# A graph network kernel: ACT and DVE swap two scalings, and the scatter takes its turn once for four groups

## The chip, the cores and the metric

The kernel runs on one core of a Trainium2 chip. The metric is the device time of one execution in microseconds (us). The engines are PE (TensorE, matrix products and transposes into PSUM), DVE (VectorE), ACT (ScalarE), POOL (GpSimd, here used for DMAs with an index per row) and SP (SyncE, here used to issue plain DMAs). Each engine works through its own instructions in order and waits on semaphores.

## The reference, cut to what matters

`x` has 100,000 rows of 128 numbers (f32). There are 25,000 edges, sorted by `dst`; `dst` is about 100,000 u^2 for uniform u, so the edges crowd at low rows.

```python
x = _layernorm(x + _L0_gnn_ref(x, edge_index, ...))   # edge MLP on x[src], x[dst]; segment_max over dst
x = _layernorm(x + _L1_gnn_ref(x, edge_index, ...))
# _L1: agg = segment_sum(x[src], dst); h = x + agg
#      res + relu(h @ W1 + b1) @ W2 + b2,  res = x @ Wres + bres
```

A row that is no edge's `dst` takes no part in the maximum or the sum: for it the two layers are plain dense products. A row that is a `dst` needs both.

## The kernel before

The kernel computes the whole output first as if no row were a `dst` (the dense work), computes the true rows of the `dst` rows in a second strand (the edge work), and lets POOL scatter these over the output rows that the dense work has stored.

**Dense work.** A unit is 512 rows (4 tiles of 128 rows, 128x512 f32). There are 196 units, four to a body, 49 bodies (0 to 48). For unit k the steps are: SP loads it into `x_in` (4 slots; slot k is loaded again when `x1_done` says that the unit in it has been scaled); DVE takes statistics (`bn_a`, `mv_a`), ACT the square root (`sd_a`), DVE the reciprocal (`rs_a`) and scales to `x1` (`norm1_scale`, L712, through the helper `scale`, L680); PE transposes to `psT`, ACT copies to `xT`; PE makes `psH`, ACT applies ReLU to `hT`; PE makes the rows in `psY` (2 buffers); DVE statistics (`bn_b`, `mv_b`), ACT root (`sd_b`), DVE reciprocal (`rs_b`), and ACT scales from `psY` to `o_rows` (`finish`, L1117, four instructions, one for each tile); SP stores. `psY` is free again at `o_done`. The layer norm needs no mean, since centring is folded into the weights. Units are pipelined: in step k DVE works on the second norm of unit k-3 and on the first norm of units k+1 to k+3, in the order that `dense` (L743) writes out.

**Edge work.** The edges are 49 groups of 512. `walk` (L310) puts each stage's edge steps beside dense units, the same for every engine:

- body 0 alone, then stage S (bodies 1 to 13, one edge step beside one unit, `step_s`): for each edge it finds where its source stands among the `dst` rows. Meanwhile POOL gathers the rows `x[src]` of groups 0 to 37 and `x[dst]` of groups 0 to 3 with indirect DMAs, four to a group.
- stage A (bodies 14 to 19, two edge steps beside one unit, an even and an odd one, `step_a`): the first layer, a running maximum, layer norm; the result goes to a table in DRAM, `x1e_table`. POOL gathers the other rows; the `dst` rows of group g wait for PE's transposes of group g-4.
- stage B (bodies 20 to 31, one edge step beside one unit, `step_b`): running sum, second layer, layer norm (`finish1`); results in `edge_rows`, counted by `res_done`. Before it can run, POOL must gather from `x1e_table`, 49 x 4 indirect DMAs (L586), which wait for the whole table.
- stage C (bodies 32 to 48): dense units alone.

After its gathers POOL scatters the 49 groups to `out` (L593), four indirect DMAs of 128 rows each to a group. Before group g it waits for `res_done` and, since the scatter must land on top of the dense rows, for the stores up to the body that holds the group's last `dst` row. That number comes from the data: `stores_16` has for each whole group 16 times this body's number, and `stores_needed` loads it into a register while the group before is scattered. After every second indirect DMA POOL waits for its descriptors to be written (`issued_pair`).

Of the kernel before, what the change touches and what calls it, by code (L numbers as in the profile page):

```python
# [36 lines left out]
TILES = 4  # L37
ROWS = TILES * P
SLOTS = 4
# [5 lines left out]
def gnn_program(nc, x, src, dst, e_w1, e_b1, e_w2, e_b2, w1, b1, w2, b2, wres, bres, out):  # L45
# [21 lines left out]
    with ctx:  # L67
# [47 lines left out]

        WHOLE = E // ROWS
        last_dst = sb("last_dst", [1, WHOLE], I32)
        stores_16 = sb("stores_16", [1, WHOLE], I32)

# [435 lines left out]
        def _(pool):  # L555
# [78 lines left out]
            def stores_needed(g):  # L634
                earlier = pool.value_load(stores_16[0:1, g:g + 1], min_val=0, max_val=16 * LAST)
                return pool.snap(earlier + 16)
# [3 lines left out]
            for g in range(GROUPS):  # L640
                j, r = divmod(g, SLOTS)
                wait(pool, final[r], 16 * TILES * j)
                pool.wait_ge(res_done, g + 1)
                if g < WHOLE:
                    for k in range(SLOTS):
                        pool.wait_ge(stored[k], count)
                    pool.nop().then_inc(s_turn, 1)
                elif g == WHOLE:
                    for k in range(SLOTS):
                        pool.wait_ge(stored[k], 16 * BODIES)  # L650
                for t in range(TILES):
# [8 lines left out]
        def _(dve):  # L660
# [50 lines left out]

            def norm1_scale(b, k):  # L712
                b, k = unit(b, k)
                if is_unit(b, k):
                    n = b * SLOTS + k
# [21 lines left out]
            def norm2_recip(b, k):  # L737
                b, k = unit(b, k)
                if is_unit(b, k):
                    dve.wait_ge(std2_done, b * SLOTS + k + 1)  # L740
                    v.reciprocal(rs_b[:, k, :], sd_b[:, k, :]).then_inc(rstd2_done, 1)  # L741

            def dense(b, k):  # L743
# [46 lines left out]
            def step_s(j, r, b):  # L790
                norm1_ready(b, r + 2)
                norm2_stats(b, r - 3)
                compare(j, r)
                norm1_var(b, r + 2)
                find(j, r - 2)
                norm2_ready(b, r - 3)
                norm1_scale(b, r + 1)
                norm2_var(b, r - 3)
                norm1_recip(b, r + 2)
                norm1_stats(b, r + 3, range(0, 2))  # L800
                norm2_recip(b, r - 3)
                norm1_stats(b, r + 3, range(2, TILES))
                keep_places(j, r - 3)
# [87 lines left out]
            def step_a(j, r, b, h):  # L891
# [9 lines left out]
                if b is not None and h % 2 == 0:  # L901
                    k = h // 2
                    norm1_ready(b, k + 2)
                    norm2_stats(b, k - 3)
                    norm1_var(b, k + 2)
                    norm1_scale(b, k + 1)
                if b is not None and h % 2 == 1:
# [3 lines left out]
                    norm2_var(b, k - 3)  # L911
                    norm1_stats(b, k + 3)
                    norm2_recip(b, k - 3)


# [46 lines left out]
            def step_b(j, r, b):  # L962
# [4 lines left out]
                if b is not None:  # L967
                    norm1_var(b, r + 2)
                    norm2_ready(b, r - 3)
                    norm1_scale(b, r + 1)  # L970
                    norm2_var(b, r - 3)
# [8 lines left out]
                if b is not None:  # L980
                    norm1_stats(b, r + 3)

# [21 lines left out]
            norm1_var(0, 1)  # L1004
            norm1_scale(0, 0)
            norm1_recip(0, 1)
# [70 lines left out]
        def _(act):  # L1077
# [54 lines left out]
            def second_half(b, k):  # L1132
                root2(b, k - 3)
                finish(b, k - 3)

# [88 lines left out]
            def step_b(j, r, b):  # L1224
# [6 lines left out]
                if b is not None:  # L1231
                    finish(b, r - 3)
                finish1(j, r - 2)

            root1(0, 0)
            root1(0, 1)
            act.wait_ge(s_w, 16 * 11)
            walk(act, dense, nothing, step_s, nothing, step_a, nothing, step_b)


# [231 lines left out]
```

## Time and profile before

| | before |
|---|---|
| median of 3 runs | 1345.21 us (1344.24 to 1346.85) |
| the profiled execution | 1332.02 us, of which 1330.2 us are the span from the first instruction to the last |
| busy: PE, DVE, ACT, POOL | 1123.7, 1068.6, 799.8, 825.8 us |
| granted clock of PE, mean | 0.952 of 2.4 GHz |
| moved by DMA | 233.86 MB, mean 176 GB/s |

Busy times are sums over stages with different limits, so none of them says by itself what sets the end. A row of the timeline is one instruction, or several of the same line that follow each other (x4); its first number is its start in us from the start of the span, the second its duration. "<-issue" is idle time for which the profile shows no other engine or transfer.

### The profile page before, as it was taken

How to read it: one execution, taken by the hardware profiler on the slowest of the kernel's cores; microseconds unless marked ns; L12 is line 12 of the kernel's file. 1: busy time of each engine (PE TensorE's matmuls, PEld its weight loads, DVE VectorE, ACT ScalarE, POOL GpSimd, SP SyncE). 2: the span in 40 equal slices, each digit the busy share in tenths (PEclk: the TensorE clock that was granted, in tenths of full speed). 3: DMA queues.
4: the chain of work that ended last, by engine and by line, in shares of the span. 5: the costliest groups of instructions: out<-in, count | busy, mean ns of one | idle time of the engine just before them, and what ended most of it. 6: DMA issues, size and time to landing. Idle time of an engine off the chain costs nothing. (4 is left out here: it accounts for less than half of the span.)

```text
span 1330.2 us, 32137 instructions
## 1 busy us (share of the span) xinstructions
PE 1123.7 (84%) x7512; PEld 853.2 (64%) x7512; DVE 1068.6 (80%) x5491; ACT 799.8 (60%) x2305; POOL 825.8 (62%) x797
## 2 busy tenths in 40 slices
PE   2699999998888878788759999999999999999500
PEld 1577777765555545455448888888887777777400
DVE  6599999989887887898838999999987888888400
ACT  0366666666665656667526666666666777777400
POOL 5666666656666666666256666666665666655654
PEclk9899999999998999999979999999999999999855
DMA  4477777756665667666436565656564556656310
GB/s 111 141 220 214 214 220 212 222 188 195 183 208 180 199 174 210 177 205 196 141 112 191 187 185 186 185 187 187 189 190 140 177 181 190 185 181 200 103 38 28
DMA packets 160366, 233.86 MB, mean 176 GB/s; under 512 B 26815, under 2 KB 69273, under 8 KB 160284
## 3 DMA queue, kind: packets, MB, share of 16 engines
q1 hardware_dynamic: 133612, 193.69, 46.7%
q0 software_dynamic: 25088, 38.81, 11.0%
q10 hardware_dynamic: 1584, 0.53, 0.2%
q14 instruction: 62, 0.51, 0.1%
q8 instruction: 20, 0.33, 0.1%
HBM read 129.48 MB, written 90.12 MB: 165 GB/s over the span
## 5 line engine op out<-in xcount | busy, mean ns | idle before, releaser
L1277 PE MATMUL psY<-wcr,xT 128*128 128x128 f32 x1568 | 305.0, 276 | 0.0
L1276 PE MATMUL psY<-wc,hT 128*128 128x128 f32 x1568 | 304.6, 276 | 0.0
L586 POOL DMA_INDIRECT edge_rows<-x1e_table,idx x196 | 210.8, 1075 | 133.2 <-DMA edge_rows<-x1e_table,idx 77.6
L593 POOL DMA_INDIRECT out<-edge_rows,idx x196 | 202.2, 1031 | 129.5 <-issue 76.4
L586 POOL DMA_INDIRECT edge_rows<-in_x,idx x196 | 206.9, 1056 | 116.0 <-DMA edge_rows<-in_x,idx 67.3
L586 POOL DMA_INDIRECT xd_rows<-in_x,idx x196 | 203.5, 1038 | 115.9 <-DMA xd_rows<-in_x,idx 67.3
L1276 PEld LDWEIGHTS psY<-wc,hT 128*128 128x128 f32 x1568 | 255.8, 193 | 15.0 <-issue 8.3
L1123 ACT ACTIVATE o_rows<-psY,rs_b 128x128 f32<-128x128 f32 x784 | 223.0, 367 | 66.7 <-DVE rs_b L741 66.5
L1277 PEld LDWEIGHTS psY<-wcr,xT 128*128 128x128 f32 x1568 | 239.9, 193 | 0.0
L1287 PE MATMUL psH<-xT,wc 128*128 128x512 f32 x392 | 204.5, 604 | 16.0 <-DVE deltas L787 10.6
L1103 ACT ACTIVATE sd_a<-mv_a,eps_col 128x4 f32<-128x4 f32 x196 | 58.3, 298 | 239.6 <-DVE mv_a L677 239.6
L672 DVE BATCH_NORM_STATS2 bn_b<-psY 128x6 f32<-128x128 f32 x784 | 174.4, 285 | 21.9 <-PE psY L1277 7.9
L691 DVE BATCH_NORM_STATS2 bn_a<-x_in 128x6 f32<-128x128 f32 x784 | 173.1, 271 | 0.3 <-DMA x_in<-in_x 0.3
L1267 PEld LDWEIGHTS psT<-ident,x 128*128 128x128 f32 x784 | 99.5, 143 | 106.2 <-issue 104.9
L1092 ACT ACTIVATE hT<-psH,bias_cols 128x512 f32<-128x512 f32 x196 | 131.0, 669 | 5.0 <-PE psH L1287 5.0
L682 DVE TENSOR_TENSOR x<-x_in,rs_a 128x512 f32<-128x512 f32 x196 | 130.6, 666 | 0.3 <-PE psT L1267 0.3
L1267 PE MATMUL psT<-ident,x 128*128 128x128 f32 x784 | 119.5, 276 | 0.9 <-DVE idx L1055 0.9
L1267 PE MATMUL psE<-ident,xs_rows 128*128 128x128 f32 x392 | 61.8, 281 | 60.8 <-ACT ehT L1161 51.6
L1100 ACT COPY xT<-psT 128x512 f32<-128x512 f32 x196 | 112.5, 574 | 0.5 <-PE psT L1267 0.5
L1267 PEld LDWEIGHTS psE<-ident,xs_rows 128*128 128x128 f32 x392 | 45.9, 143 | 98.2 <-issue 83.0
L923 DVE TENSOR_TENSOR_SCAN shared<-mask,shared,psE 128x512 f32<-128x512 bf16 x48 | 61.4, 1279 | 36.5 <-PE psE L1267 23.5
L1287 PEld LDWEIGHTS psH<-xT,wc 128*128 128x128 f32 x392 | 65.8, 194 | 35.6 <-issue 11.0
(135 smaller groups left out, 2042.6 us busy)
## 6 DMA issues: line engine op xcount, KB each, us to landing
x_in<-in_x SPq DMA_DIRECT2D x196, 256.0 KB
out<-o_rows SPq DMA_DIRECT2D x196, 256.0 KB
xs_rows<-edge_rows SPq DMA_DIRECT2D x98, 256.0 KB, 2.9
xs_rows<-src_dram SPq DMA_DIRECT2D x49, 256.0 KB, 4.3
mask<-mask_dram SPq DMA_DIRECT2D x98, 128.0 KB, 3.6
x1e_table<-shared SPq DMA_DIRECT2D x49, 256.0 KB, 2.8
x1eT_spill<-x1eT SPq DMA_DIRECT2D x49, 256.0 KB
x1eT<-x1eT_spill SPq DMA_DIRECT2D x49, 256.0 KB, 2.8
```

Source lines behind the costliest of these rows:

```text
L586: nc.gpsimd.indirect_dma_start(to, None, table, bass.IndirectOffsetOnAxis(idx[:, what, t:t + 1], 0), bounds_check=rows - 1, oob_is_err=err ...
L593: nc.gpsimd.indirect_dma_start(table, bass.IndirectOffsetOnAxis(idx[:, SCAT, t:t + 1], 0), frm, None, bounds_check=N - 1, oob_is_err=False ...
L672: last = v.bn_stats(bn[:, t, :], rows[:, cut(t)])
L682: v.tensor_tensor(tiles(to), tiles(rows), rs.unsqueeze(2).broadcast_to([P, TILES, P]), ALU.mult).then_inc(done, 1)
L691: last = v.bn_stats(bn_a[:, k % 2, t, :], x_in[:, k, cut(t)])
L1092: a.activation(hT[:, k % 2, :], psH[:, :], ACT.Relu, bias=bias_cols[:, 2:3]).then_inc(hT_done, 1)
L1100: a.copy(xT[:, k, :], psT[:, :]).then_inc(xT_done, 1)
L1123: last = a.activation(o_rows[:, k, cut(t)], psY[k % 2][:, cut(t)], ACT.Copy, scale=rs_b[:, k, t:t + 1])
L1267: last = t_.transpose(to[:, cut(t)], rows[:, cut(t)], ident[:, :])
L1276: t_.matmul(to[:, cut(t)], h[:, cut(t)], wc2[:, :], start=False, stop=False, skip_group_check=True)
L1277: last = t_.matmul(to[:, cut(t)], xt[:, cut(t)], wcr[:, :], start=False, stop=t == TILES - 1, skip_group_check=True)
L1287: t_.matmul(psH[:, :], wc1[:, :], xT[:, k, :], start=True, stop=True).then_inc(w1_done, 1)
```

## The change

Two edits. First, the scalings are swapped. ACT now makes `x1` from `x_in` with four instructions, after the root for the second norm; DVE now makes `o_rows` from `psY` with one instruction (`scale`), at the end of its step, after the reciprocal `rs_b`. The statistics of the next unit move up to where DVE's scaling stood. Second, POOL's scatter takes its turn (the four waits on `stored`, the nop, and the register load) only at every fourth group, with the count of the last group of the four.

```diff
             def stores_needed(g):
-                earlier = pool.value_load(stores_16[0:1, g:g + 1], min_val=0, max_val=16 * LAST)
+                top = g + SLOTS - 1
+                earlier = pool.value_load(stores_16[0:1, top:top + 1], min_val=0, max_val=16 * LAST)
                 return pool.snap(earlier + 16)
...
                 pool.wait_ge(res_done, g + 1)
-                if g < WHOLE:
+                if g < WHOLE and r == 0:
                     for k in range(SLOTS):
                         pool.wait_ge(stored[k], count)
                     pool.nop().then_inc(s_turn, 1)
...
                 for t in range(TILES):
-                    if t == TILES - 1 and g + 1 < WHOLE:
+                    if t == TILES - 1 and r == SLOTS - 1 and g + 1 < WHOLE:
                         count = stores_needed(g + 1)
```

DVE:

```diff
-            def norm1_scale(b, k):
-                    dve.wait_ge(rstd1_done, n + 1)
-                    wait(dve, t_done, n - 1)
-                    scale(x1[:, k % 2, :], x_in[:, k, :], rs_a[:, k, :], x1_done)
+            def finish(b, k):
+                    dve.wait_ge(rstd2_done, b * SLOTS + k + 1)
+                    wait(dve, stored[k], 16 * b)
+                    scale(o_rows[:, k, :], psY[k % 2], rs_b[:, k, :], o_done)
 
             def dense(b, k):
                 norm1_ready(b, k + 2)
                 norm2_stats(b, k - 3)
                 norm1_var(b, k + 2)
                 norm2_ready(b, k - 3)
-                norm1_scale(b, k + 1)
+                norm1_stats(b, k + 3, range(0, 1))
                 norm2_var(b, k - 3)
                 norm1_recip(b, k + 2)
-                norm1_stats(b, k + 3, range(0, 2))
+                norm1_stats(b, k + 3, range(1, TILES))
                 norm2_recip(b, k - 3)
-                norm1_stats(b, k + 3, range(2, TILES))
+                finish(b, k - 3)
```

`step_s`, `step_a` and `step_b` of DVE are changed in the same way: in stage A two of the four statistics take the scaling's place in the even step, and `finish` comes last in the odd step; in stages S and B `finish` comes after the last statistics (in S ahead of `keep_places`). The first `norm1_scale(0, 0)` moves to ACT too.

ACT:

```diff
-            def finish(b, k):
-                    act.wait_ge(rstd2_done, b * SLOTS + k + 1)
-                    wait(act, stored[k], 16 * b)
+            def norm1_scale(b, k):
+                    act.wait_ge(rstd1_done, n + 1)
+                    wait(act, t_done, n - 1)
                     for t in range(TILES):
-                        last = a.activation(o_rows[:, k, cut(t)], psY[k % 2][:, cut(t)], ACT.Copy,
-                                            scale=rs_b[:, k, t:t + 1])
-                    last.then_inc(o_done, 1)
+                        last = a.activation(x1[:, k % 2, cut(t)], x_in[:, k, cut(t)], ACT.Copy,
+                                            scale=rs_a[:, k, t:t + 1])
+                    last.then_inc(x1_done, 1)
...
             def second_half(b, k):
                 root2(b, k - 3)
-                finish(b, k - 3)
+                norm1_scale(b, k + 1)
```

## Rows read from the trace of the kernel before

**Rows 1.** Windows of three stretches: us, each engine's busy time and count, granted clock, DMA.

```profile
668.00:990.00 322.00, 307.85 (x2103) 254.06 (x2102) 271.07 (x1362) 203.36 (x632) 210.76 (x196) 0.97 0.57 179
990.00:1255.00 265.00, 255.71 (x1729) 202.03 (x1727) 222.75 (x1374) 201.35 (x603) 161.59 (x155) 1.00 0.56 175
1255.00:1331.00 76.00, 0.00 (x0) 0.00 (x0) 0.00 (x0) 0.00 (x0) 40.58 (x42) 0.50 0.11 33
```

**Rows 2.** Waits of the whole span: in total, times, longest us.

```profile
POOL edge_rows L586 <- DMA x1e_table<-shared: 22.8, 1, 22.8
DVE bn_z L672 <- PE psE L1267: 21.1, 25, 1.7
```

**Rows 3.** Timeline of POOL near the end: start, us, [idle before <-releaser].

```profile
1290.21 0.98 POOL L593 DMA_INDIRECT out<-edge_rows,idx  x1 [1.10 <-issue]
...
1309.49 0.98 POOL L593 DMA_INDIRECT out<-edge_rows,idx  x1 [1.08 <-issue]
...
1315.65 0.98 POOL L593 DMA_INDIRECT out<-edge_rows,idx  x1 [0.81 <-DMA out<-edge_rows,idx]
```

**Rows 4.** Timeline of DVE and POOL in stage C.

```profile
1094.20 0.89 DVE L672 BATCH_NORM_STATS2 bn_b<-psY 128x6 f32<-128x128 f32 x4
...
1095.29 0.69 DVE L682 TENSOR_TENSOR x<-x_in,rs_a 128x512 f32<-128x512 f32 x1
...
1095.43 1.41 POOL L593 DMA_INDIRECT out<-edge_rows,idx  x1 [0.81 <-DMA out<-edge_rows,idx]
...
1096.98 0.18 DVE L741 RECIPROCAL rs_b<-sd_b 128x4 f32<-128x4 f32 x1 [0.28 <-ACT sd_b L1103]
...
1097.65 0.49 DVE L672 BATCH_NORM_STATS2 bn_b<-psY 128x6 f32<-128x128 f32 x2
```

**Rows 5.** Timeline of DVE and POOL in stage B, early and late.

```profile
694.71 0.69 DVE L934 TENSOR_TENSOR xsT<-shared,x1eT 128x512 f32<-128x512 f32 x1
...
694.86 1.41 POOL L586 DMA_INDIRECT edge_rows<-x1e_table,idx  x1 [0.30 <-issue]
...
894.04 0.66 DVE L934 TENSOR_TENSOR xsT<-shared,x1eT 128x512 f32<-128x512 f32 x1
...
894.57 1.00 POOL L586 DMA_INDIRECT edge_rows<-x1e_table,idx  x1 [0.81 <-DMA edge_rows<-x1e_table,idx]
...
897.58 0.66 DVE L682 TENSOR_TENSOR x<-x_in,rs_a 128x512 f32<-128x512 f32 x1
...
897.67 1.43 POOL L586 DMA_INDIRECT edge_rows<-x1e_table,idx  x1 [0.81 <-DMA edge_rows<-x1e_table,idx]
```

**Rows 6.** Timeline of DVE and POOL in stage A.

```profile
594.42 0.20 DVE L855 RECIPROCAL rs_e<-sd_e 128x8 f32<-128x8 f32 x1
...
594.66 0.69 DVE L682 TENSOR_TENSOR shared<-psE,rs_e 128x512 f32<-128x512 f32 x1
594.85 1.01 POOL L586 DMA_INDIRECT xd_rows<-in_x,idx  x1 [0.79 <-DMA xd_rows<-in_x,idx]
...
595.29 1.28 DVE L876 TENSOR_TENSOR_SCAN shared<-mask,shared,psE 128x512 f32<-128x512 bf16 x1
```

**Rows 7.** Timeline of DVE over one unit of stage S.

```profile
201.09 0.89 DVE L672 BATCH_NORM_STATS2 bn_b<-psY 128x6 f32<-128x128 f32 x4
...
204.88 0.18 DVE L741 RECIPROCAL rs_b<-sd_b 128x4 f32<-128x4 f32 x1
204.98 0.46 DVE L691 BATCH_NORM_STATS2 bn_a<-x_in 128x6 f32<-128x128 f32 x2
...
205.56 0.89 DVE L672 BATCH_NORM_STATS2 bn_b<-psY 128x6 f32<-128x128 f32 x4
```

**Rows 8.** Groups of ACT by form: busy, mean ns | idle before.

```profile
L1123 ACT ACTIVATE o_rows<-psY,rs_b 128x128 f32<-128x128 f32 x784 | 223.0, 367 | 66.7 <-DVE rs_b L741 66.5 <-issue 0.2
...
L1178 ACT ACTIVATE edge_rows<-xs_rows,rs_e 128x128 f32 x128 | 41.0, 400 | 0.0
```

**Rows 9.** DMA issues: KB each, median us to landing.

```profile
x1eT<-x1eT_spill SPq DMA_DIRECT2D x49, 256.0 KB, 2.8
```

More of the change, by code:

```diff
@@ L116, in gnn_program @@
         WHOLE = E // ROWS
+        assert WHOLE % SLOTS == 0
         last_dst = sb("last_dst", [1, WHOLE], I32)
@@ L710, in norm1_recip @@
                     v.reciprocal(rs_a[:, k, :], sd_a[:, k, :]).then_inc(rstd1_done, 1)
-            def norm1_scale(b, k):
-                b, k = unit(b, k)
-                if is_unit(b, k):
-                    n = b * SLOTS + k
-                    dve.wait_ge(rstd1_done, n + 1)
-                    wait(dve, t_done, n - 1)
-                    scale(x1[:, k % 2, :], x_in[:, k, :], rs_a[:, k, :], x1_done)
             def norm2_stats(b, k):
@@ L741, in norm2_recip @@
                     v.reciprocal(rs_b[:, k, :], sd_b[:, k, :]).then_inc(rstd2_done, 1)
+            def finish(b, k):
+                b, k = unit(b, k)
+                if is_unit(b, k):
+                    dve.wait_ge(rstd2_done, b * SLOTS + k + 1)
+                    wait(dve, stored[k], 16 * b)
+                    scale(o_rows[:, k, :], psY[k % 2], rs_b[:, k, :], o_done)
             def dense(b, k):
@@ L796, in step_s @@
                 norm2_ready(b, r - 3)
-                norm1_scale(b, r + 1)
+                norm1_stats(b, r + 3, range(0, 1))
                 norm2_var(b, r - 3)
                 norm1_recip(b, r + 2)
-                norm1_stats(b, r + 3, range(0, 2))
+                norm1_stats(b, r + 3, range(1, TILES))
                 norm2_recip(b, r - 3)
-                norm1_stats(b, r + 3, range(2, TILES))
+                finish(b, r - 3)
                 keep_places(j, r - 3)
@@ L905, in step_a @@
                     norm1_var(b, k + 2)
-                    norm1_scale(b, k + 1)
+                    norm1_stats(b, k + 3, range(0, 2))
                 if b is not None and h % 2 == 1:
@@ L911, in step_a @@
                     norm2_var(b, k - 3)
-                    norm1_stats(b, k + 3)
+                    norm1_stats(b, k + 3, range(2, TILES))
                     norm2_recip(b, k - 3)
+                    finish(b, k - 3)
             def segment_sum(j, r):
@@ L969, in step_b @@
                     norm2_ready(b, r - 3)
-                    norm1_scale(b, r + 1)
+                    norm1_stats(b, r + 3, range(0, 1))
                     norm2_var(b, r - 3)
@@ L980, in step_b @@
                 if b is not None:
-                    norm1_stats(b, r + 3)
+                    norm1_stats(b, r + 3, range(1, TILES))
+                    finish(b, r - 3)
             v.memset(eps_col[:, :], EPS)
@@ L1004, in _ @@
             norm1_var(0, 1)
-            norm1_scale(0, 0)
             norm1_recip(0, 1)
@@ L1115, in root2 @@
                     root(sd_b[:, k, :], mv_b[:, k, :, :], std2_done)
-            def finish(b, k):
+            def norm1_scale(b, k):
                 b, k = unit(b, k)
                 if is_unit(b, k):
-                    act.wait_ge(rstd2_done, b * SLOTS + k + 1)
-                    wait(act, stored[k], 16 * b)
+                    n = b * SLOTS + k
+                    act.wait_ge(rstd1_done, n + 1)
+                    wait(act, t_done, n - 1)
                     for t in range(TILES):
-                        last = a.activation(o_rows[:, k, cut(t)], psY[k % 2][:, cut(t)], ACT.Copy,
-                                            scale=rs_b[:, k, t:t + 1])
-                    last.then_inc(o_done, 1)
+                        last = a.activation(x1[:, k % 2, cut(t)], x_in[:, k, cut(t)], ACT.Copy,
+                                            scale=rs_a[:, k, t:t + 1])
+                    last.then_inc(x1_done, 1)
             def first_half(b, k):
@@ L1231, in step_b @@
                 if b is not None:
-                    finish(b, r - 3)
+                    norm1_scale(b, r + 1)
                 finish1(j, r - 2)
@@ L1236, in _ @@
             root1(0, 1)
+            norm1_scale(0, 0)
             act.wait_ge(s_w, 16 * 11)
```

## The prediction

> **What bounds the kernel now.** I read the windows first, then who waited for whom, then POOL's and DVE's timelines side by side. The reader should see that dense work doesn't set the end. From 1255 us on PE, DVE and ACT are idle, and only POOL's indirect DMAs run, 42 of them [rows 1]. Before that POOL runs its 196 gathers from the edge table back to back from 668 to 990, and its 196 scatters follow without a pause [rows 1]. It last waited long for others at 668, 22.8 us for the table's stores [rows 2]; in the code it also waits for stage A's first transposes before it gathers further `dst` rows. So the span is: the end of stage S (it lets stage A begin), stage A up to the table's last store, and then 392 indirect DMAs of POOL. Dense units after 668 only have to stay ahead of the scatters.
>
> A POOL issue has a natural price. With nothing beside it it takes 0.98 us, the next pair follows after 0.81 us, and the next group of four after 1.08 us; only at the last group is that 0.81 too, though it waits for the four `stored` counts, as constants [rows 3]. In the gathers it is 1.00, with 0.30 inside a pair [rows 5]. While DVE works, some issues last longer. In stage C one that starts 0.14 us into `x<-x_in,rs_a` lasts 1.41 [rows 4]; in stage B one that starts 0.09 us into it lasts 1.43 [rows 5]. Both end 0.86 us after DVE's instruction does (1096.84 against 1095.98, 899.10 against 898.24): POOL's issue stands until DVE is through.
>
> **The change, part by part.**
>
> *One turn for four groups.* Of the 49 scatter groups, 36 lose four register waits, the nop, and the register load ahead of them. If their gap goes from 1.08 to 0.81 [rows 3], that is 36 x 0.27 = 9.7 us, all on POOL's chain. Bounds: zero if the `res_done` wait, which stays, carries the cost, and 9.7. The last group has that wait too, at 0.81, so I take 9.7. In return the first group of each four waits for the output rows of the group three further on. The latest such turn is group 44's, at 1290.2 [rows 3]; it would need what edge 24575 needs: row 100000 x (24576/25000)^2 = 96,600, body 47 (bodies 0 to 48). Dense work was over before 1255 [rows 1], and body 47 four units of 3.45 us earlier [rows 4], near 1240. That cover is 50 us; what eats it comes below.
>
> *DVE's x1 scaling goes, and POOL is freed of it.* What replaces it on DVE reads PSUM and one small SBUF operand. Stage A has that form now: a POOL issue that starts 0.19 us into `shared<-psE,rs_e` lasts 1.01 us, not lengthened [rows 6]. So `finish` should not hold POOL. In stage C the lengthening is 161.59 - 155 x 0.98 = 9.7 us [rows 1], and nothing else in a dense unit reads two SBUF tensors: -9.7. Bounds: 0 (the PSUM form blocks too) and -12, a quarter more, since gaps beside it may be stretched as well.
>
> In stage B it is 210.76 - 196 x 1.00 = 15 us [rows 1], but I don't book it. Four gathers take by nature 4 x 1.00 + 0.30 + 0.81 + 0.30 + 0.81 = 6.2 us; POOL took 322/49 = 6.57 us [rows 1], and that is also the pitch of a step of stage B, which PE fills (307.85 us busy of 322). POOL is being held to DVE's period: each step it comes 0.37 us earlier, runs into `x<-x_in,rs_a`, and is pushed back by as much. Stage B has a second instruction with two SBUF tensors, `xsT<-shared,x1eT` (L934), and that lengthens too: an issue 0.15 us into it lasted 1.41 [rows 5]. Today POOL starts 0.53 us into it and just escapes, at 1.00 [rows 5]. With the first blocker gone POOL slides 0.37 us earlier and falls into the second, which at 0.66 us is long enough to hold it for good. At most five steps pass until one of four starts meets it: 5 x 0.37 = 1.9 us. I take -2; bounds 0 and -15.
>
> Here a rule can be weighed. The rows show issues escaping or being held until DVE's end, and where they fall isn't chance but a slide [rows 5]. The Trainium skill, "SBUF — State Buffer", section "Who interferes with whom", says that a DVE instruction with two SBUF inputs contends with a GpSimd instruction that reads SBUF, and that the one to start second blocks fully; it says nothing of who meets whom. Were POOL's starts spread at random, the 0.66 us left in each step would cost 4 x 0.66/6.57 x 0.33 = 0.13 us a group, 6.5 us in all, and stage B would gain 9 us rather than 2. By that reading the time would be 7 us lower.
>
> *DVE in stage S.* Its instructions stand back to back; a unit takes 201.09 to 205.56 = 4.47 us [rows 7]. It pays 0.69 us for the PSUM form and loses 0.66 for the SBUF one [rows 5, 6]. `finish` also waits for the reciprocal just ahead of it: that step is 0.24 us in stage A [rows 6], against 0.10 from the reciprocal to the next statistics now [rows 7]. Together +0.17 us. Against it, the wait of the next step for DVE's own last statistics (205.44 to 205.56) would be met early: up to -0.15. So +0.02 to +0.17 a unit, over 52 units +1 to +9. I take +3, since the gap that goes is seen directly. The reverse, a shorter stage S, would need PE to be faster, and PE is full there too; I give it no weight.
>
> *ACT.* Four scalings from SBUF at 0.40 us each take the place of four from PSUM at 0.37 [rows 8], some 0.1 us a unit. ACT was busy 201 of 265 us in stage C [rows 1], less elsewhere, and no longer waits for `rs_b`. Cost 0; if ACT had no slack, 196 x 0.1 = 20 us. x1 is there some 2 us later in its step; PE transposes it a step later, which covers that.
>
> *Stage A.* 0. DVE waited 21.1 us in 25 places, 0.84 each, for `bn_z`'s input [rows 2]; `finish` comes just ahead of those, after two statistics fewer. The even steps' chain, DVE's `mv_a` to ACT's root, ReLU and copy, is untouched. Without that cover: 24 x 0.63 = 15 us.
>
> *Stage C's dense work* gets longer, off the path. A unit is 1094.20 to 1097.65 = 3.45 us, in a loop from `bn_b` through ACT to `rs_b` and in 0.67 us back to `bn_b` [rows 4]. That leg becomes 0.24 + 0.63 = 0.87 [rows 6], so 3.65 a unit; 68 units add 14 us. Body 47 is stored near 1240 + 14 + 3 (stage S) + 3 (landing) = 1260. POOL comes to group 44 at 1290.2 - 9.7 - 2 - 33 x 0.27 + 3 = 1273. 13 us are left: hidden.
>
> **Sum.** -9.7 (turn) - 9.7 (stage C) - 2 (stage B) + 3 (stage S) = -18.4 us. The profiled execution took 1332.0 us; the runs shown have a median of 1345.2, 13 us above it, an offset that I let stand. 1345.2 - 18.4 = 1326.8, say 1326.
>
> **Rivals.**
> 1. *POOL runs free in stage B too.* For: L934 hits it rarely so far. Against: those hits look the same. 13 us more; POOL is then at group 44 at 1260, just as body 47's rows land: 1313. Chance 0.13.
> 2. *Stage S slows by 0.3 us a unit*, DVE waiting for `std2` behind ACT's queue. For: ACT's root comes after ReLU and copy. Against: three statistics, not two, now lie in that wait. 52 x 0.3 = 16 instead of 3: 1339. Chance 0.13.
> 3. *The PSUM form blocks POOL as well*, so half of the change doesn't do what I say. Against: rows 6. -9.7 and +3 are left: 1338. Chance 0.07.
> 4. *Slower: the stores become the end.* Place: group 44's turn. x1 releases its input slot 2 us later, the reload comes late, and a unit of stage C stretches beyond 3.65. From 3.85 (0.2 x 64 = 13 us) POOL waits, from 4.15 the gain is gone, at 4.3 it is 1326 + 29 = 1355. For: the reload keeps about 4.4 us, two units less the 3 by which it is late. Against: other transfers of this size land in 2.8 [rows 9]. Chance 0.06.
> 5. *Stage A pays for `finish` in full and more*, 24 x 1 us: 1350. Against: the waits in front of `bn_z`. Chance 0.06.
>
> The forecast case has 0.5, with its own range of 1318 to 1332; 0.05 is left for what I don't see. A measurement of this kernel tells about 0.2%, 2.7 us, from no change. Faster by more: 0.5 + 0.13 + 0.12 (of case 2) + 0.06 and a little of the rest, 0.82; within: 0.06; slower: 0.12. The range takes in cases 1 to 3: 1310 to 1341.
>
> **What would show it.** Right: scatter gaps of 1.08 at every fourth group and 0.81 at the others; issues of 1.0 us through stage C; in stage B still 6.6 us a group, the long issues now beginning inside L934; stage S 1 to 9 us longer; a dense unit of stage C near 3.65. Wrong: gathers at 6.2 us a group (case 1), a unit of stage S over 4.7 (2), POOL's issues lengthened inside `o_rows<-psY` (3), POOL waiting for `out<-o_rows` at group 44 (4), the table's last store more than 10 us after 668 with stage S unchanged (5).

## The result and the profile after

| | time, us | kernel before, same chip | ratio, 95% |
|---|---|---|---|
| the change, first measured | 1383.01 (1373.12 to 1387.28, 4 runs) | 1346.03 | 1.0274 (1.0219 to 1.0328) |
| the change, measured again later (e11) | 1331.60 (1328.67 to 1334.96, 10 runs) | 1334.28 | 0.9981 (0.9967 to 0.9995) |

The change was slower by 2.7% when it was first measured, where 1326 us was forecast. The same kernel on another occasion was 0.2% faster than the kernel before. Both are true, and most of this document is about what lies between them: TensorE's semaphore updates, which on some occasions arrive microseconds late.

The first profiled execution took 1383.84 us, 1381.8 of them span. Windows of it over stage B, the dense part of C, and the end (columns as in [rows 1]):

```profile
715.00:1089.00 374.00, 333.27 (x2231) 268.41 (x2230) 288.67 (x1453) 221.63 (x678) 237.15 (x236) 0.98 0.54 164
1089.00:1334.00 245.00, 228.85 (x1474) 171.12 (x1473) 197.60 (x1218) 174.03 (x512) 124.83 (x127) 1.00 0.55 168
1334.00:1381.00 47.00, 13.88 (x99) 11.37 (x97) 11.98 (x60) 8.18 (x22) 19.67 (x20) 0.69 0.19 65
```

Before, DVE and PE were through at 1255 and POOL went on alone [rows 1]. Now dense work runs past 1334, and in its last part POOL does little. Its waits (in total, times, longest) and its timeline say why:

```profile
POOL out L594 <- DMA out<-o_rows: 56.1, 3, 53.9
POOL edge_rows L587 <- DMA x1e_table<-shared: 36.4, 1, 36.4
DVE bn_y L675 <- remote: 30.3, 23, 3.1
DVE bn_b L675 <- remote: 18.7, 18, 2.3
```

```profile
1287.69 0.98 POOL L594 DMA_INDIRECT out<-edge_rows,idx  x1 [0.50 <-issue]
1342.58 0.98 POOL L594 DMA_INDIRECT out<-edge_rows,idx  x1 [53.91 <-DMA out<-o_rows]
1343.86 0.98 POOL L594 DMA_INDIRECT out<-edge_rows,idx  x1 [0.30 <-issue]
```

That is the turn of group 44: POOL stood 53.9 us for output rows that dense work had not stored. What POOL itself does became shorter, as the change meant. What became longer is everything that PE feeds. Where the stages begin (first `hT<-psH` of the stage, first and last indirect DMA, us from the span's start):

| | before | after | after again (e11) | turn, exchange in C alone, marks (e17) |
|---|---|---|---|---|
| stage S | 59.8 | 64.9 | 63.9 | 59.9 |
| stage A | 301.9 | 320.8 | 309.7 | 302.9 |
| stage B | 684.1 | 715.5 | 704.2 | 688.3 |
| stage C | 1016.6 | 1089.4 | 1038.6 | 1023.6 |
| first gather from the table | 668.2 | 699.8 | 689.1 | 672.5 |
| first scatter | 991.4 | 1009.7 | 1009.6 | 996.8 |
| last scatter | 1320.0 | 1371.6 | 1316.9 | 1305.0 |
| span | 1330.2 | 1381.8 | 1327.0 | 1315.2 |

Stage B took 373.9 us instead of 332.5. Its unit was 6.6 us before; now, but for one, units of 6.1 to 9.5 follow each other without order. By its own execution stage C began 72.8 us later than before: the start of stage S gave 5.1 of it, stage S 13.8, stage A 12.5 and stage B 41.4. "<-remote" in the waits is a semaphore update that fits the end of no instruction in the profile. It stands only at waits for what PE makes, on DVE above all (`bn_b`, `bn_y`). The table was ready late too, 36.4 us of waiting for 22.8 [rows 2].

**How a late update looks.** The trace has the time of a semaphore update beside the end of the instruction that carries it. In the first profile of before, all 1053 updates of PE that stages S to C show lie within 0.04 us of that end. After the change, of those recorded, 141 of 236 in stage S, 6 of 183 in A, 180 of 260 in B and 46 of 154 in C come more than 0.3 us behind the last matmul that carries one, up to 5.6 us; those of ACT and DVE are never over 0.01 us late. A piece of experiment e3, from the trace (start, duration, instruction; `update` rows are semaphores):

```
1210.57 0.28 PE  last matmul psY<-wcr,xT  (carries y_done)
1211.66      PE  psH<-xT,wc, ends 1212.78 (carries w1_done)
1212.95 0.27 PE  last transpose of psT    (carries t_done)
1212.97      update x1_done (ACT, on time)
1215.15      update y_done   4.31 us behind its matmul
1215.18 0.30 DVE bn_b<-psY
1215.19      update w1_done  2.41
1215.25      update t_done   2.03
```

PE worked on: the product and the transposes behind the late one are in the record, and a product of 1.12 us can't have been done in the 0.04 us between the first two updates. So it is the word of the work that is late, and it comes in a bunch. It isn't only the time noted for it: DVE, which waits for this update, starts 0.03 us after that time. All that comes behind DVE's first wait stands too:

```profile
1212.14 0.69 DVE L685 TENSOR_TENSOR o_rows<-psY,rs_b 128x512 f32<-128x512 f32 x1
1215.18 0.50 DVE L675 BATCH_NORM_STATS2 bn_b<-psY 128x6 f32<-128x128 f32 x2 [2.34 <-remote]
```

**Missing records go with it.** The six traces without a late update (before, e8 to e11, e17) hold 29,921 to 30,676 semaphore updates, those of the DMAs included. The 13 with many late ones hold 12,335 to 14,139, and e7 holds 19,886. Records of every engine are missing. In stage C they are missing only while POOL issues: in those 13 traces 62% to 73% of the updates of PE, DVE and ACT are there then, and practically all while POOL waits. So what delays PE's updates also loses records, or the recording is itself what delays them. Every execution on record has its span and granted clock noted, so no run here tells the two apart.

### The profile page after: what moved, and what is told of

It is laid out like the page before. It is cut to its first block and busy times, and to the rows that moved or that the text cites. A ratio compares the mean times of both kernels' runs of the same rounds, so it can differ in the third digit from the quotient of the medians.

```text
span 1381.8 us, 31908 instructions
## 1 busy us (share of the span) xinstructions
PE 1171.4 (85%) x7512; PEld 861.5 (62%) x7512; DVE 1082.8 (78%) x5491; ACT 807.2 (58%) x2305; POOL 797.4 (58%) x797
## 5 line engine op out<-in xcount | busy, mean ns | idle before, releaser
L1281 PE MATMUL psY<-wc,hT 128*128 128x128 f32 x1568 | 308.5, 279 | 0.0
L594 POOL DMA_INDIRECT out<-edge_rows,idx x196 | 194.3, 991 | 170.7 <-issue 94.3
L587 POOL DMA_INDIRECT edge_rows<-x1e_table,idx x196 | 197.3, 1007 | 146.8 <-issue 90.2
L1281 PEld LDWEIGHTS psY<-wc,hT 128*128 128x128 f32 x1568 | 259.8, 196 | 19.6 <-issue 11.6
L587 POOL DMA_INDIRECT edge_rows<-in_x,idx x196 | 201.6, 1029 | 116.0 <-issue 73.6
L1127 ACT ACTIVATE x<-x_in,rs_a 128x128 f32<-128x128 f32 x784 | 249.5, 394 | 0.0
L694 DVE BATCH_NORM_STATS2 bn_a<-x_in 128x6 f32<-128x128 f32 x784 | 179.5, 271 | 5.1 <-DMA x_in<-in_x 5.0
L1272 PEld LDWEIGHTS psT<-ident,x 128*128 128x128 f32 x784 | 91.3, 143 | 147.3 <-issue 91.8
L685 DVE TENSOR_TENSOR o_rows<-psY,rs_b 128x512 f32<-128x512 f32 x196 | 134.8, 688 | 9.6
L1095 ACT ACTIVATE hT<-psH,bias_cols 128x512 f32<-128x512 f32 x196 | 131.6, 671 | 12.5 <-PE psH L1292 6.4
L1272 PE MATMUL psT<-ident,x 128*128 128x128 f32 x784 | 125.2, 283 | 14.3 <-ACT x L1127 6.6
```

What stands on the lines that cost most here:

```text
L587: nc.gpsimd.indirect_dma_start(to, None, table, bass.IndirectOffsetOnAxis(idx[:, what, t:t + 1], 0), bounds_check=rows - 1, oob_is_err=err ...
L594: nc.gpsimd.indirect_dma_start(table, bass.IndirectOffsetOnAxis(idx[:, SCAT, t:t + 1], 0), frm, None, bounds_check=N - 1, oob_is_err=False ...
L685: v.tensor_tensor(tiles(to), tiles(rows), rs.unsqueeze(2).broadcast_to([P, TILES, P]), ALU.mult).then_inc(done, 1)
L694: last = v.bn_stats(bn_a[:, k % 2, t, :], x_in[:, k, cut(t)])
L1095: a.activation(hT[:, k % 2, :], psH[:, :], ACT.Relu, bias=bias_cols[:, 2:3]).then_inc(hT_done, 1)
L1127: last = a.activation(x1[:, k % 2, cut(t)], x_in[:, k, cut(t)], ACT.Copy, scale=rs_a[:, k, t:t + 1])
```

## The experiments

Late updates are given as "late/recorded" for stages S, B and C (C to the end of the span), from the one profiled execution of each kernel. "Chip" is the median of the kernel before in the same batch on the same chip. An occasion with late updates is called disturbed here, one without them quiet. Where no ratio stands, the kernel's own runs spread too far for one (e0 is a single run).

| | kernel | us | chip | ratio, 95% | S | B | C |
|---|---|---|---|---|---|---|---|
| e1 | turn alone | 1359.2 | 1365.6 | 0.995 (0.991 to 0.998) | 148/238 | 146/252 | 6/184 |
| e2 | exchange alone | 1421.0 | 1365.6 | | 176/250 | 191/257 | 38/137 |
| e3 | after, x1 first | 1489.6 | 1365.6 | | 164/246 | 213/271 | 53/183 |
| e4 | after, reciprocal apart | 1475.7 | 1365.6 | 1.081 (1.077 to 1.084) | 157/235 | 182/263 | 74/188 |
| e0 | before | 1339.5 | 1340.4 | | 119/216 | 115/241 | 14/186 |
| e5 | after, both on DVE | 1351.3 | 1340.4 | 1.009 (1.006 to 1.012) | 61/208 | 26/207 | 21/183 |
| e6 | after, both on ACT | 1373.7 | 1340.4 | 1.028 (1.022 to 1.034) | 152/219 | 120/228 | 54/160 |
| e7 | after, pause behind each issue | 1498.6 | 1340.4 | 1.118 (1.113 to 1.124) | 27/198 | 0/208 | 0/135 |
| e8 | after, mark on each issue | 1332.2 | 1334.3 | 0.999 (0.997 to 1.001) | 0/257 | 0/290 | 0/198 |
| e9 | turn, mark on each issue | 1331.0 | 1334.3 | 0.997 (0.996 to 0.998) | 0/251 | 0/290 | 0/202 |
| e10 | after, pause in the scatters | 1388.2 | 1334.3 | 1.041 (1.039 to 1.043) | 0/260 | 0/290 | 0/199 |
| e11 | after | 1331.6 | 1334.3 | 0.998 (0.997 to 1.000) | 0/261 | 0/290 | 0/196 |
| e12 | turn, exchange in C alone | 1408.9 | 1365.0 | 1.034 (1.029 to 1.039) | 149/234 | 156/250 | 75/187 |
| e13 | exchange alone | 1424.6 | 1365.0 | 1.046 (1.040 to 1.052) | 165/243 | 180/269 | 41/143 |
| e14 | after, A as before | 1466.4 | 1365.0 | 1.073 (1.067 to 1.079) | 159/235 | 215/269 | 55/190 |
| e15 | turn alone | 1361.3 | 1365.0 | 0.999 (0.995 to 1.003) | 163/242 | 132/241 | 6/193 |
| e16 | as e12 | 1396.6 | 1362.1 | | 134/229 | 124/239 | 91/176 |
| e17 | as e12, mark on each issue | 1314.0 | 1334.7 | 0.985 (0.983 to 0.986) | 0/260 | 0/290 | 0/201 |

### First batch: which edit, and is x1 or DVE's scaling late?

e1 and e2 are the two edits of the change, each alone. e3 moves ACT's job to the head of its step; it still makes unit k+1 there, so it comes a step earlier:

```diff
             def first_half(b, k):
+                norm1_scale(b, k + 1)
                 root1(b, k + 2)
...
                 root2(b, k - 3)
-                norm1_scale(b, k + 1)
```

e4 puts work between DVE's reciprocal and the scaling that waits for it:

```diff
-                norm1_stats(b, k + 3, range(1, TILES))
+                norm1_stats(b, k + 3, range(1, 3))
                 norm2_recip(b, k - 3)
+                norm1_stats(b, k + 3, range(3, TILES))
                 finish(b, k - 3)
```

e1: 

> The kernel before, with the scatters turning once for four groups and no job exchanged. Both theories below put the loss on the exchange of jobs, so both expect what the prediction's term for the turn says: 36 turns less of about 0.27 us, 9.7 us, so 1333 to 1338 us. A rival: the turn moved to the first group of four asks for stores that land up to four groups later, so that the last turn (group 44) waits for the dense stores also without the exchange. Then 1342 us or more, and the trace shows a wait of POOL of several us at group 44.

e2: 

> The kernel after, with a turn for every group as before. If the exchange is what costs, 1375 to 1393 us (the kernel after, with at most 10 us more, and nothing more if POOL waits for stores at the end anyway). If the turn is what costs (its wait asks for stores of later groups), about 1336 us.

e3: 

> The kernel after, with ACT scaling x1 as the first thing of its step instead of the last. Theory X (x1 comes just in time for TensorE's transposes, and TensorE, full in stages S and B, loses each wait): TensorE's waits on ACT's x1 (61 us in 95 pieces) vanish, stage S's unit of 5.6 us in each loop turn goes back to 4.5, stage B's unit to near 6.6, total about 1320 to 1340 us. Theory D (it is DVE's output scaling from PSUM at the end of its step, behind its own reciprocal, that delays y's buffer and DVE's next step): no more than 10 us are won, 1372 to 1383 us, and stage B's unit stays at 7.5 or more.

e4: 

> The kernel after, with DVE's reciprocal of norm 2 one statistics instruction earlier in the dense steps and in stage S, so that its output scaling doesn't wait for the instruction just ahead of it. Theory D: the unit of 5.6 us in each loop turn of stage S and the irregular units of stage C shrink, 1360 to 1372 us. Theory X: nothing changes, 1378 to 1388 us.

The kernel before took 1365.6 us on this chip, 20 more than in the first measurement. The turn is innocent (0.995), the exchange costs. All four took longer than expected, on a base that was itself 20 us higher. The wait that e1's rival names is there:

```profile
POOL out L594 <- DMA out<-o_rows: 4.1, 1, 4.1
```

But e1 has 148 late updates in stage S and 146 in B, and its stage C began at 1090.1 us, 73.5 later than in the profile of before: dense work came late to the turn, not the turn early. Both theories of the exchange's cost fell: x1 a step earlier took PE's waits for it away and the kernel still became slower, and so did the one with the reciprocal apart. Neither touches anything that could cost 50 to 70 us. What they have in common is DVE waiting for "remote", in total, times, longest, in e3:

```profile
DVE bn_b L675 <- remote: 91.2, 58, 3.2
DVE bn_y L675 <- remote: 44.1, 28, 3.1
```

The update times above came out of looking for that. e3 also shows when they are on time. In its stage C, windows of one unit each:

```profile
1206.01:1210.46 4.45, 4.34 (x33) 3.59 (x32) 3.14 (x21) 2.71 (x9) 2.94 (x3) 1.00 0.66 174
1210.46:1216.59 6.13, 3.94 (x27) 2.99 (x25) 3.15 (x22) 2.71 (x10) 3.93 (x4) 1.00 0.58 188
1307.64:1311.23 3.59, 3.57 (x25) 2.81 (x25) 3.05 (x21) 2.71 (x8) 0.00 (x0) 1.00 0.52 146
1311.73:1315.47 3.74, 3.63 (x26) 2.88 (x25) 3.11 (x21) 2.71 (x9) 0.00 (x0) 1.00 0.54 145
```

While POOL issues (fifth busy time above 0), a unit takes 3.6 to 6.1 us. POOL waits for the stores twice, 35.6 us ahead of group 40 (from 1294) and 94.1 us ahead of group 44; there (POOL at 0.00) all units but the first take 3.59 to 3.73 us until the work runs out. Of the 105 updates of PE recorded more than 1.5 us into these two waits none is late. It is the same in all ten traces with such a wait of over 4 us (the kernel after, e1 to e4, e6, e12 to e14, e16): 0 of 556.

### Second batch: is it the kernel before's too, and what brings it?

e0 is the kernel before. e5 is the kernel after with `norm1_scale` on DVE in its old place, so DVE has both scalings; e6 has `finish` back on ACT, behind `norm1_scale`. e7 makes POOL wait for each of its issues:

```diff
-                if issued[0] % 2 == 0:
-                    kw["engine_sem"] = s_issued
+                kw["engine_sem"] = s_issued
...
-                if issued[0] % 2 == 0:
-                    pool.wait_ge(s_issued, issued[0] // 2)
+                pool.wait_ge(s_issued, issued[0])
```

e0: 

> The kernel before once more, on this chip, for its trace. New theory L: TensorE's semaphore updates arrive late (by 1 to 8 us, several in one bunch) while GpSimd issues its indirect DMAs, and each late one holds DVE and ACT; the exchange makes this more frequent, the queue itself is not slower. If the kernel before suffers from it too and only its first profiled execution was free of it, this trace has some 150 late updates in each of stages S and B and nearly none in C, and the time is 1345 to 1370 us, not 1332. If lateness comes only with the changed kernels, it has none.

e5: 

> The kernel after with x1's scaling back on DVE at its old place: DVE has both scalings, ACT neither. If it is DVE's two-operand read of SBUF (which lengthens GpSimd's issues and locks their rhythm to the units) that keeps TensorE's updates in time in stage C, this kernel has few late updates there (under 10 of some 180), while its unit is set by DVE at 3.9 to 4.2 us; total 1375 to 1400 us. If the scaling of the output on DVE brings the lateness, C has 40 or more late updates here as after the change.

e6: 

> The kernel after with the output scaling back on ACT, behind x1's: ACT has both, DVE neither. ACT is then full (stage C's unit about 4.3 us by ACT's 2.7 us and 1.6 us more, stage B's about 7), total 1400 to 1440 us. If the freed GpSimd is the source of the lateness, late updates of TensorE stay in stage C (30 or more) though DVE no longer touches the output; if DVE's scaling is the source, there are under 10.

e7: 

> The kernel after, but GpSimd waits for the end of each indirect issue, not of every second one: a group of four goes from 6.2 to about 7.2 us, so stages B and C can be held by GpSimd, but it is quiet for longer. Theory L: the late updates come out in the pause behind a pair (0.5 to 0.8 us after its end in two of three cases), so with a pause behind each issue the longest delays fall from 5 to 6 us to under 3, the units of S and B become more even, and the total is 1340 to 1375 us. If the lateness has nothing to do with GpSimd's issuing, the total is 1383 us or more.

The kernel before has late updates too, in S and B, and hardly in C: its first profiled execution (1332.0 us) had none, and the median of its other runs was 13 us above. e0's 1339.5 us lie below the 1345 to 1370 expected. e5 is better than expected (1351.3 us, not 1375 or more): DVE sets the unit (S 4.91, C 3.83 us, nearly all alike), PE has time left in each, and fewer updates are late, 21 of 183 in C, which is between the two cases that I had set. e6 was faster than expected too, and has 54 of 160 late in C although ACT scales the output, so DVE's PSUM scaling is not what brings them; what e6, the kernel after, and e2 to e4 share is that x1's scaling has left DVE. e7's total was missed by far: 7.2 us a group was too slow for the gathers of stages A and B (A took 463 us). But its late updates are as theory L says: none in A, B and C, and none over 1.2 us in S. The occasion was a disturbed one all the same, since records are missing here too: only 208 of PE's 290 updates in B and 135 of 202 in C are there, where all but a few are in the traces of quiet occasions. So the lateness can be kept away while whatever loses the records goes on. Units of C are 3.58 to 3.75 us with POOL issuing beside them:

```profile
1202.06 0.98 POOL L592 DMA_INDIRECT out<-edge_rows,idx  x1 [0.81 <-DMA out<-edge_rows,idx]
1203.86 0.98 POOL L592 DMA_INDIRECT out<-edge_rows,idx  x1 [0.81 <-issue]
```

### Third batch: the mark or the pause, and stage C

e8 and e9 keep e7's first edit (each issue marks its end) and wait for every second one; e8 from the kernel after, e9 from before with the turn. e10 has e7's pause in the last 196 issues alone. e11 is the kernel after.

e8: 

> The kernel after, with GpSimd marking the end of every indirect issue (as the run that waited for each issue did) but waiting only for every second one (as the kernel after does). It separates the mark from the pause. If it is the pause behind each issue that lets TensorE's updates through, this kernel is as late as the kernel after: 100 or more late updates in each of S and B, its time within 1.5% of the kernel after. If it is the mark, the late updates are gone in A, B and C at GpSimd's full pace of 6.2 us a group, and the time falls to 1310 to 1340 us.

e9: 

> The kernel before with one turn for four groups and every issue marked, waiting for every second one. If the pause matters and not the mark: as the turn alone, 0.993 to 0.997 of the kernel before. If the mark matters: 0.975 to 0.985, since late updates cost the kernel before some 25 us in S and B.

e10: 

> The kernel after, with GpSimd waiting for each issue in the scatters alone (last 196 of its 784); the gathers keep their pairs. Theory L: stage C's units become even (3.59 to 3.75 us, mean 3.65 against 3.85) with no late update there, S and B stay as late as in the kernel after; 68 units by 0.2 us are 13 us, and GpSimd's 49 groups of 7.2 us end just as the dense stores do, so 1365 to 1378 us where the kernel after takes 1383. If lateness comes from elsewhere, C stays uneven and the time is 1383 us or more.

e11: 

> The kernel after once more, on the chip of these runs, so that traces and times of one chip can be compared. Theory L: 1.02 to 1.04 of the kernel before, again with late updates of TensorE above all in S and B, and some 40 in C.

This was the chip of the first batch, 25 minutes later, and nothing was late in any of the four, so e11 missed its 1.02 to 1.04. The kernel before took 1334.3 us on it, not 1365.6. So the lateness isn't the chip's, nor the kernel's alone: something that changes with time turns it on. Mark against pause couldn't be told apart. e10 shows the bare price of the pause, 365.6 us of scatters for 307.3, and gains nothing where nothing is late (1388.2 us, above the range expected).

e11 is the measurement of the change that the prediction can be held against step by step. In stage B a gather that starts 0.14 us into `xsT<-shared,x1eT` is held:

```profile
803.75 0.66 DVE L937 TENSOR_TENSOR xsT<-shared,x1eT 128x512 f32<-128x512 f32 x1
...
803.89 1.38 POOL L587 DMA_INDIRECT edge_rows<-x1e_table,idx  x1 [0.81 <-DMA edge_rows<-x1e_table,idx]
```

In stage C nothing holds an issue, and the unit is 3.60 to 3.75 us:

```profile
1095.09 0.69 DVE L685 TENSOR_TENSOR o_rows<-psY,rs_b 128x512 f32<-128x512 f32 x1
1095.36 0.98 POOL L594 DMA_INDIRECT out<-edge_rows,idx  x1 [0.81 <-DMA out<-edge_rows,idx]
```

Stage A is where the gain goes. Two of its units each in e9 (A's jobs as before) and in e11:

```profile
426.89:441.60 14.71, 12.46 (x69) 8.27 (x67) 13.12 (x60) 9.93 (x28) 9.53 (x10) 1.00 0.66 203
441.60:456.38 14.78, 12.42 (x69) 8.29 (x67) 13.08 (x60) 9.86 (x27) 10.07 (x10) 1.00 0.66 198
```

```profile
438.72:455.05 16.33, 14.18 (x67) 9.41 (x67) 13.28 (x60) 10.10 (x28) 10.86 (x11) 0.90 0.60 186
455.05:469.83 14.78, 12.60 (x67) 8.21 (x67) 13.26 (x60) 9.97 (x27) 9.36 (x9) 1.00 0.65 200
```

The unit of 16.33 us has a granted clock of 0.90, the others 1.00, and PE is busy 1.6 us longer over the same work. PE's timeline, e9 and then e11, has the idle time ahead of it:

```profile
440.73 1.04 PE L1269 MATMUL psE<-ident,shared 128*128 128x128 f32 x8
443.47 0.63 PE L1269 MATMUL psE<-ident,xs_rows 128*128 128x128 f32 x4 [1.71 <-ACT ehT L1163]
```

```profile
437.46 1.09 PE L1272 MATMUL psE<-ident,shared 128*128 128x128 f32 x8
440.60 0.63 PE L1272 MATMUL psE<-ident,xs_rows 128*128 128x128 f32 x4 [2.05 <-ACT ehT L1165]
441.07 0.63 PE L1272 MATMUL psE<-ident,xd_rows 128*128 128x128 f32 x4
441.54 1.50 PE L1386 MATMUL psE<-ehT,raw 128*128 128x512 f32 x2
```

PE's longest wait in two steps, for ACT's ReLU, is 1.71 us in e9 and 2.05 in e11. After it, in e11, the granted clock falls to 0.5 (1.2 GHz) and two products take 1.50 us instead of 1.02. Of e11's 20 waits of 1.88 to 2.05 us at this place 12 are followed by such a fall; of the 37 of 1.47 to 1.78 us in e9 and before none is. Stage A has 17 such stretches in e11, 68 us together, against 5 with 27 us in e9 and 6 with 34 in before. The sizes fit. From one first `hT<-psH` to the next, nine of e11's 24 units in stage A take 16.25 to 16.66 us, each with one fall, and one each in e9 and before; most others take 14.6 to 15.0 us in all three. Eight units by 1.6 us are 13 us, and stage A grew by 12.4. e5 and e6 tell which half of the exchange does it: with DVE scaling the output (e5) 16 stretches, with ACT doing both (e6) 5, and stage A took 389.3 and 383.4 us.

### Fourth and fifth batch: the exchange in stage C alone

e12 has the turn, and the exchange in the dense steps after body 0 alone; e14 is the kernel after with both jobs in stage A as before. e13 and e15 are e2 and e1 again.

```diff
             def dense(b, k):
+                late = not (isinstance(b, int) and b == 0)
...
-                norm1_scale(b, k + 1)
+                if late:
+                    norm1_stats(b, k + 3, range(0, 1))
+                else:
+                    norm1_scale(b, k + 1)
```

e12: 

> The kernel before with the turn for four groups, and the exchange of jobs in the steps of stage C alone; S, A and B as before. Theory K (the exchange costs in A by TensorE's clock, in S and B by fuller queues, and gives in C by GpSimd's freed issues): scatters begin where they did before (about 992 us), take 307 us as after the change and not 326, so the span is 1309 us and the time 1311 us, ratio 0.980 to 0.986 on a quiet chip. If the gain in C hangs on something in the other stages, 0.995 or more. With late updates of TensorE (a kernel before above 1340 us): 0.985 to 1.005, since C's units then have 13 us of slack before the turn of group 44.

e13: 

> The exchange alone, a turn for every group, once more on this chip. Quiet chip: the kernel after and 36 turns more of 0.27 us, so 1339 to 1343 us, ratio 1.003 to 1.008; stage A has 10 or more stretches of half clock. With late updates: 1.03 to 1.05 as at first.

e14: 

> The kernel after with stage A's jobs as in the kernel before. Theory K: stage A goes from 394.6 us back to 382, with 5 or fewer stretches of half clock, and the time falls by 10 to 13 us to 1319 to 1322 us, ratio 0.988 to 0.991 on a quiet chip. If A is slow for another reason (x1 late, more work on DVE in S), it stays at 390 us or more and the ratio at 0.998.

e15: 

> One turn for four groups alone, once more on this chip. In the run with marks GpSimd's groups in stage C stayed at 6.87 us, two units of DVE, since DVE's two-operand scaling holds the issues to the units' rhythm, and the turn's 9.7 us were mostly lost to longer issues (54 over 1.2 us, not 14). So 0.995 to 0.998, not 0.993.

Here the kernel before took 1365.0 us, and updates were late again. e12 is then 1.034, outside the range I gave: stage C alone had 75 of 187 updates late, all before POOL stood at group 44.

```profile
POOL out L594 <- DMA out<-o_rows: 83.9, 2, 82.8
DVE bn_b L675 <- remote: 77.0, 49, 3.9
```

Beside it e15, the same kernel but for stage C's jobs, had 6 of 193 late in C and units of 3.36 to 3.49 us, one excepted. That pair shows what the exchange does in C when updates can be late. e14's stage A fell from e13's 12 stretches of half clock to 7, but took 394.0 us against 394.9. It had more late updates in A too (46 of 215 against 25 of 198), so it doesn't settle A. The turn alone is worth little, since POOL's groups stay at two units of DVE, 6.9 us, with 55 issues held over 1.2 us.

e16: 

> The exchange in stage C alone with the turn for four groups, once more. Quiet chip (kernel before at 1331 to 1338 us): S, A and B as in the kernel before, scatters of 307 us in place of 326, time 1311 to 1318 us, ratio 0.980 to 0.988, no late update. Disturbed chip (kernel before at 1350 us or more): 1.03 again, with uneven units in C while GpSimd issues and even ones while it waits.

e17: 

> The exchange in stage C alone, the turn for four groups, and a mark on every indirect issue with a wait for every second one. Quiet chip: 1311 to 1318 us, ratio 0.980 to 0.988. Disturbed chip: if the pause behind each issue is what helps, stage C is uneven as in the two runs before (ratio 1.02 to 1.04, 40 or more late updates in C); if the mark is, C is even (3.59 to 3.75 us) and the ratio 0.98 to 1.00.

e16 met late updates again (1396.6 us for 1362.1, about 1.025). e17 met none and gave 0.985 (0.983 to 0.986), the version that the experiments pointed to, within the 1311 to 1318 us expected. Its windows, stage B, dense C, end:

```profile
684.00:1023.00 339.00, 328.61 (x2247) 269.93 (x2247) 289.59 (x1462) 219.52 (x682) 221.37 (x206) 0.98 0.57 178
1023.00:1270.00 247.00, 238.53 (x1570) 180.95 (x1568) 205.28 (x1266) 181.05 (x533) 153.65 (x157) 1.00 0.57 177
1270.00:1315.00 45.00, 0.59 (x6) 0.40 (x4) 2.92 (x12) 0.41 (x2) 23.15 (x24) 0.55 0.14 44
```

It beats the kernel before when updates are on time, and by its ratio the kernel after too. Its marks have no part in that: the kernel after gave 0.999 with them (e8) and 0.998 without (e11). With late updates only the version without marks was seen, and it was as bad as the change (e12, e16). So neither can be called the better kernel without knowing how often that is, and e17's own time with late updates is not known.

## Why the prediction was wrong

**What failed for the first measurement: the base.** "13 us above it, an offset that I let stand": I took the difference between the profiled execution (1332.0 us) and the median (1345.2) for a constant. It was most likely the kernel's own loss to late updates. The profiled execution had none. Where traces show none, the kernel before had medians of 1334.3 and 1334.7 us; where they show many, 1340.4 to 1365.6. For the executions behind 1345.2 there is no trace, so for them this is inferred. And the loss is no constant, it grows when x1's scaling leaves DVE: the kernel after takes 1383.0 us with late updates and 1331.6 without, 51 us where before has 12 (1346.0 against 1334.3).

**And the overlap.** "Dense units after 668 only have to stay ahead of the scatters", with 13 us left at group 44, "hidden", and nothing booked for it. The forecast let stage C begin 3 us later and gave it units of 3.65 us. It began 72.8 us later, and its first 56 units took 3.85 us on average. POOL was ready for group 44 at 1288.7 and stood until 1342.6, 53.9 us for nothing forecast. All terms of the sum were on POOL's chain, and for the first measurement that chain wasn't what ended last. No rival had late updates. Rival 4 named the right place, POOL at group 44, and a wrong cause: `x_in`'s reload cost DVE 5 us in 5 waits; the units were stretched by PE's late word, and most of the delay was there before stage C began.

**Step by step, against the execution without late updates** (e11's against before's):

- *Stage S, +3:* 242.1 to 245.7 us, +3.6. Right.
- *Stage B, -2, POOL relocked by L934:* 320.2 to 317.0 us of gathers, -3.2, at 6.59 us a group. Right, mechanism too: of 39 issues that begin inside that instruction (now L937) all but two are held, 13 us together. Rival 1, POOL free at 6.2, came only with late updates, when the units no longer keep a rhythm.
- *Turn and stage C's contention, -19.4 together:* scatters from 328.7 to 307.3 us, -21.4. Right, in both parts: the issues themselves became 9.7 us shorter together, none longer than 1.11 us, and the idle time between them 11.7. Gaps of 1.08 to 1.10 are left at every fourth group, the others are 0.81 or 0.82, but for one. They aren't independent, though: with x1's scaling on DVE the turn's 9.7 us are mostly lost to longer issues (e9: 325.9 us of scatters).
- *Dense unit of stage C 3.65 us:* 3.59, 3.60, 3.69, 3.74 in turn, mean 3.65. Right, and hidden.
- *Stage A, 0:* 382.2 to 394.6 us, +12.4. Wrong, and this is the term that failed where nothing was late. I looked at DVE's waits ahead of `bn_z` for room and not at PE, whose idle time in that stage grew by 0.3 us to a length behind which its clock fell. Rival 5 had the place with 0.06.
- *Not in the sum:* stage S begins 4.2 us later, since the first units, with the pipeline still empty, now have ACT's four scalings in their chain. With body 0 as before (e12, e16, e17) it begins at 59.2 to 60.2. That the scalings are the reason is argued from the code.

The forecast gain was 18.4 us; without late updates it was 3.2 by the spans, and 12.4 + 4.2 of the missing 15.2 are stage A and the start, with small terms of the other sign beside them.

**What stays open.** What turns the lateness on, and by what way POOL's issues delay PE's word and nobody else's. That POOL's issues are needed is shown by the waits in which POOL stands (0 of 556 late) and by e7. Whether the recording of the semaphores takes part is not known, since no run was made without it. In about two of three cases the first update of a bunch comes 0.5 to 0.8 us behind the end of an issue, or as the next one starts. Why x1's scaling on DVE protects stage C (6 to 21 late of 183 to 193 in e0, e1, e5 and e15, 28% to 52% in the kernel after, e2 to e4, e6, e12 to e14 and e16) was only argued: it locks POOL's issues to the units, and they may then miss each other. Whether e7's mark or its pause keeps the updates on time was not decided. That stage A's cost would go in the kernel after with A's jobs undone was seen only through e17, e5 and e6, not by e14.

## What to carry to other kernels

When a profiled execution is 1% faster than the median, find out what it lacks before using it as the base: here it had none of the late updates that made the difference. Before giving an engine on a chain one more instruction, look at the idle gaps of PE behind it, since a gap that grew by 0.3 us here cost 1.6 us through the clock in more than half of its cases. Measure a change on more than one occasion when its kernel leans on GpSimd's indirect DMAs; 1.027 and 0.998 were the same code.

## What the runs showed of the hardware

- TensorE's semaphore updates can arrive over 9 us behind the matmul that carries them (9.49 in e14, and DVE's `bn_b` starts 0.02 us after it), in bunches, while those of ACT and DVE are within 0.01 us (one of DVE's 0.14). The matmuls behind go on. In the traces that show this, more than half of all semaphore updates are missing from the record, and what part recording has in it is open. The Trainium skill, "TensorE: Matmul & The Clock Gate", section "Why this matters for your kernels", prices an update in tens of nanoseconds; the executions without late ones agree (within 0.07 us), the others don't.
- The same chip had the kernel before at 1365.6 us and 25 minutes later at 1334.3.
- In stage A the granted clock fell to 0.5 (1.2 GHz) behind 12 of 20 idle gaps of 1.88 to 2.05 us (e11), and behind none of 37 gaps of 1.47 to 1.78 us at the same place (e9 and before); e14 and e6 have one fall each behind 1.71 and 1.50 us. A unit of 14.8 us became 16.3.
- An issue of POOL held by DVE's two-SBUF instruction ends 0.86 us after that instruction, whichever of the two (803.89 + 1.38 against 803.75 + 0.66), as in [rows 4, 5].
